# A gated attention and a causal attention with experts on one core: features by halves of the tokens, and half of the gathered work moved into the second part

## What is computed

```python
q, k, v = split(x @ w_qkv.T)                      # 16 heads of 64
dots = einsum('bhid,bhjd->bhij', q, k) * 64**-0.5
gate = soma_gate(q.mean(axis=heads))              # layer norm over 64, linear, gelu, linear,
                                                  # top 32 of 512 tokens per batch kept, sigmoid
dots = dots * (gate[:, None, :, None] * gate[:, None, None, :])
x = layernorm(x + softmax(dots) @ v @ w_out.T + b_out)
```

```python
x1 = x + mla(rmsnorm(x, g1))       # 16 heads of 8, keys and values through a latent of 64, causal softmax
x2 = x1 + moe(rmsnorm(x1, g2))     # 8 experts of 256, top 2 by gate logits, silu
x = layernorm(x + x2)
```

## Time and profile before

| | us |
|---|---|
| three runs | 715.31, 706.88, 701.70 (median 706.88) |
| profiled execution | 699.82, span 698.1 |
| busy: PE, DVE, ACT, POOL | 645.9, 491.2, 419.5, 256.5 |
| mean granted clock of PE | 0.976 |
| end of part one (last matmul, last copy) | 73.4, 73.8 |

### The profile page before, as it was taken

One profiled execution on the slowest core, in us unless ns is written; L12 is line 12 of the kernel. 1 busy time (PEld: TensorE's weight loads), 2 busy tenths in 40 slices (PEclk: granted clock), 3 DMA queues, 4 the chain that ended last, 5 costly groups with the idle time before them and its releaser, 6 DMA issues.

```text
span 698.1 us, 13992 instructions
## 1 busy us (share of the span) xinstructions
PE 645.9 (93%) x5388; PEld 429.9 (62%) x5388; DVE 491.2 (70%) x1043; ACT 419.5 (60%) x753; POOL 256.5 (37%) x321
## 2 busy tenths in 40 slices
PE   7689689889899999999999999999999999989985
PEld 2367444455456666666666766767676667756765
DVE  2557456865777778877887788768777877764775
ACT  2543254666577666766685768666857575664432
POOL 3632301221243344343532543343334343533433
PEclk9899798999999999999999999999999999999999
DMA  8500000000000000000000000000000000000000
GB/s 318 178 0 32 1 1 1 2 1 1 1 1 2 1 1 1 16 2 1 1 17 1 1 2 16 1 1 3 16 1 1 2 17 1 1 1 16 1 16 15
DMA packets 9923, 12.15 MB, mean 17 GB/s; under 512 B 1593, under 2 KB 8194, under 8 KB 9602
## 3 DMA queue, kind: packets, MB, share of 16 engines
q1 hardware_dynamic: 9106, 11.25, 4.8%
q10 hardware_dynamic: 752, 0.01, 0.1%
HBM read 9.16 MB, written 2.10 MB: 16 GB/s over the span
## 4 chain that ended last, share of the span: by engine, by line
PE 69%; DVE 10%; ACT 5%; issue 3%; POOL 2%; POOLq 0%; ACTq 0%; DVEq 0%
PE turn L964 15%; PE turn L957 11%; PE psV L1017 11%; PE psW L1005 9%; PE psS L990 6%; PE turn L919 5%; PE turn L909 3%; DVE negmax L1198 3%; PE psS L979 2%; ACT prob L1117 2%; PE turn L927 2%; ACT X L1036 1%; PE turn L938 1%; DVE qs L1207 1%; PE turn L872 1%
## 5 line engine op out<-in xcount | busy, mean ns | idle before, releaser
L1117 ACT ACTIVATE prob<-psW 128x1024 f32<-128x1024 f32 (+1 forms) x192 | 182.9, 953 | 109.5 <-PE psW L1005 109.1
L1198 DVE TENSOR_REDUCE negmax<-psS 128x2 f32<-128x1024 f32 (+2 forms) x249 | 198.7, 818 | 31.5 <-PE psS L990 31.0
L841 POOL TENSOR_SCALAR_AFFINE_SELECT prob<-prob 128x512 f32<-128x512 f32 x128 | 80.0, 638 | 280.0 <-ACT prob L1117 280.0
L1258 DVE SCALAR_TENSOR_TENSOR late<-late,turn 128x512 f32<-128x512 f32 x128 | 87.5, 684 | 66.3 <-ACT late L1087 65.6
L964 PE MATMUL turn<-wexp,late 128*128 128x128 f32 x1024 | 128.0, 278 | 1.5 <-DVE late L1258 1.3
L964 PEld LDWEIGHTS turn<-wexp,late 128*128 128x128 f32 x1024 | 119.6, 192 | 9.6 <-issue 6.0
L1087 ACT ACTIVATE late<-turn 128x512 f32<-128x512 f32 x128 | 76.4, 598 | 60.7 <-PE turn L957 57.9
L1005 PE MATMUL psW<-qT,kT 26*128 26x256 f32 (+2 forms) x512 | 93.1, 400 | 8.9 <-ACT prob L1117 8.1
L849 POOL TENSOR_TENSOR late<-late 128x512 f32<-128x512 f32 x63 | 80.6, 1280 | 45.7 <-DVE late L1277 45.7
L979 PE MATMUL psS<-kT,qT 24*128 24x256 f32 (+1 forms) x498 | 90.7, 400 | 1.7 <-DVE negmax L1198 1.6
L1017 PE MATMUL psV<-prob,va 128*32 128x512 f32 (+3 forms) x1024 | 91.0, 450 | 0.2 <-POOL prob L841 0.2
(11 more groups left out here) (260 smaller groups left out, 900.8 us busy)
## 6 DMA issues: line engine op xcount, KB each, us to landing
XT<-in_xT SPq DMA_DIRECT2D x4, 512.0 KB, 6.7
X<-in_x SPq DMA_DIRECT2D x1, 2048.0 KB, 15.8
out<-late SPq DMA_DIRECT2D x8, 256.0 KB, 2.2
WQKV<-in_wqkvT SPq DMA_DIRECT2D x1, 1024.0 KB
late<-in_w SPq DMA_DIRECT2D x1, 1024.0 KB, 9.6
WQKV<-in_wqkvT SPq DMA_DIRECT2D x2, 256.0 KB, 3.7
late<-in_woutT SPq DMA_DIRECT2D x1, 512.0 KB
base_all<-base_rows SPq DMA_DIRECT2D x1, 512.0 KB, 3.8
```

What stands on the lines that cost most here:

```text
L841: pool.affine_select(out=blk, in_=blk, compare_op=ALU.is_ge, fill=0.0, base=0, pattern=[[0, 4], [1, P]], channel_multiplier=-1).then_inc(s ...
L1117: A(into, src, ACT.Exp).then_inc(s["exp_ready"], 1)
L1198: last = V.tensor_reduce(negmax[:, u % 2, c, 2 * p:2 * p + 2], scores_in(b, n)[:, :, HALF * i:HALF * i + P * (c + 1)], AX, ALU.max, negate ...
L1258: V.scalar_tensor_tensor(out=hid[:, e % 2, k, :], in0=tanh[:, n % 2, :], scalar=1.0, in1=bank("hidden", b, n)[:, :], op0=ALU.add, op1=ALU. ...
```

## The change

In part one:

- Features are made in eight passes of 256 columns: first the first 256 tokens of all four pairs of batches, then the others. Each half has banks of its own for squares and gate. The square root, reciprocal and product of the first half stand between passes.
- gcol and w1raw come first among the small loads and have a semaphore of their own (`ld_w1`, `w1_ready`). PE's sum of squares waits for neither.
- One square root on a dummy element is issued on ACT before the passes. The ten unread matmuls beside the softmax go, twelve (`IN_GATE`) come ahead of the scores.
- The gather's first half is followed at once by its base rows, queries, keys and scores; the second half of the gather and the values, slots and base rows follow beside the softmax. Base rows go through DRAM in two halves of four batches, each with its semaphores.
- The base rows of batches 3, 5, 6 and 7 are added on POOL, the others on DVE.
- The second half's queries, keys and values leave part one.

In part two, they come as six steps "half parts" right after the first "apply": four of four matmuls, two of one, each copied out by ACT. To keep what they read alive, `WQKV`, `XT`, `Xg` and `Xc` are laid into the tile `prob`. The second "apply" comes behind them. `ADD_AT` goes from 2.02 to 1.32, some other places move by up to 1.4 slots, one "unread" goes, and the last batch's last two experts (before: the last) are summed on DVE alone.

```diff
+WARM, IN_GATE, BY_POOL = 7, 12, (3, 5, 6, 7)
 # SP
-            sp.dma_start(keep["rows"], base[:, :]).then_inc(base_out, 16)
-            sp.wait_ge(base_out, 16)
-            sp.dma_start(base_all[:, :, :], keep["rows"].unsqueeze(0).broadcast_to([P, B, D])).then_inc(base_in, 16)
+            for n in range(NH):
+                rows = slice(HB * n, HB * n + HB)
+                sp.wait_ge(base_sb, n + 1)
+                sp.dma_start(keep["rows"][rows, :], base[:, n, :]).then_inc(base_out[n], 16)
+                sp.wait_ge(base_out[n], 16)
+                sp.dma_start(base_all[:, rows, :], keep["rows"][rows, :].unsqueeze(0).broadcast_to([P, HB, D])
+                             ).then_inc(base_in[n], 16)
 # POOL
-            pool.wait_ge(wc_ready, 2)
+            pool.wait_ge(w1_ready, 1)
...
-            pool.wait_ge(base_in, 16)
             pool.wait_ge(bdT_ready, 1)
-            for b in range(BY_DVE, B):
+            for b in BY_POOL:
+                pool.wait_ge(base_in[b // HB], 16)
 # PE
+            for t in range(B):
+                h, j = divmod(t, B // 2)
+                if t >= 1 and t + 1 < B:
+                    features(t + 1)
+                pe.wait_ge(f_sb, 2 * t + 2)
+                mm(var_in[h][rows_of(j), 0:HALF], ones64[:, :], sq[:, t % 2, 0:HALF], start=True, stop=True,
+                   tile_position=(0, 2 * GH * j)).then_inc(v_done, 1)
+                if t == 1:
+                    pe.wait_ge(w1_ready, 1)
+                if t:
+                    gate_rows(t - 1)
...
             pe.wait_ge(ld_w, 48)
...
+            pe.wait_ge(masks, 2)
+            pe.wait_ge(g_used, 1)
+            unread(IN_GATE)
             for i in range(2):
                 pe.wait_ge(gelu, i + 1)
...
+            gather(0)
+            pe.wait_ge(xs_sb, 1)
+            base_rows(0)
+            for g in range(4):
+                for k in range(4):
+                    last = mm(bank[g][:, P * k:P * k + P], WQKV[:, at:at + P], Xg[:, 0:P], start=True, stop=True)
+                last.then_inc(qk_ps, 1)
...
+            pe.wait_ge(w1_scaled, 1)
+            gather(1)
+            for k in range(2):
+                mm(bank[(6, 4)[k]][:, :], Xc[:, 0:P], WQKV[:, 2 * INNER + 512 * k:2 * INNER + 512 * k + 512],
+                   start=True, stop=True).then_inc(v_ps, 1)
             for n in range(NH):
-                last = mm(bank[(4, 6)[n]][:, :], selh[:, n, :], slot[:, :], start=True, stop=True)
+                last = mm(bank[2 + n][:, :], selh[:, n, :], slot[:, :], start=True, stop=True)
             last.then_inc(sr_ps, 1)
             pe.wait_ge(base_sb, 1)
-            values(0, (bank[7], bank[5]))
-            other = [bank[k] for k in (2, 3, 0, 1)]
-            queries_keys(1, other, range(2))
-            pe.wait_ge(s_shift, 1)
-            queries_keys(1, other, range(2, 4))
-            pe.wait_ge(qk1_sb, 1)
-            for i in range(IN_SOFTMAX):
-                mm(bank[2][:, :], keep["identb"][:, :], keep["maskb"][:, :], start=True, stop=True)
+            pe.wait_ge(xm_ready, 1)
+            base_rows(1)
             pe.wait_ge(bdT_ready, 1)
...
-            values(1, (bank[4], bank[6]))
 # places in part two (some)
-GATE_AT, SUM_AT, ADD_AT = 1.0, 1.21, 2.02
+GATE_AT, SUM_AT, ADD_AT = 1.0, 1.21, 1.32
-EARLY = {0: -40.35, 1: -38.0}
+EARLY = {0: -40.35, 1: -37.2}
+    ("half parts", 0): -40.25, ("half parts", 1): -40.15, ("half parts", 2): -40.05, ("half parts", 3): -39.95,
+    ("half parts", 4): -39.85, ("half parts", 5): -39.75,
-("half turned", 1): 11.5
+("half turned", 1): 13.5
 # the new step on PE
+                elif what == "half parts":
+                    if n < 4:
+                        for k in range(4):
+                            at = P * (4 * n + k)
+                            last = mm(into[:, P * k:P * k + P], WQKV[:, at:at + P], Xg[:, P:2 * P], start=True, stop=True)
+                    else:
+                        last = mm(into[:, :], Xc[:, P:2 * P], WQKV[:, 512 * n:512 * n + 512], start=True, stop=True)
+                    last.then_inc(is_full(*step), 1)
 # POOL's adds and DVE's sums
-                elif what == "add" and (b, n) != (B - 1, NE - 1):
+                elif what == "add" and (b < B - 1 or n < NE - 2):
-                    if (b, n) == (B - 1, NE - 1):
+                    if b == B - 1 and n >= NE - 2:
```

More of the change, by code:

```diff
@@ L298, in _ @@
             last.then_inc(wvo_ps, 1)
-            pe.wait_ge(ld_next, 16 * len(keep["loads"]))
-            mm(bank[5][:, 0:2 * D], keep["wd"][:, :], keep["wu"][:, :, :], start=True, stop=True).then_inc(wqk_ps, 1)
-            def unread(count):
-                for i in range(count):
-                    mm(bank[6][:, :], keep["identb"][:, :], keep["maskb"][:, :], start=True, stop=True)
-            pe.wait_ge(masks, 2)
             for i in range(TOPK // 8):
@@ L716, in causal_attention_and_experts @@
         negmax = sb("negmax", [P, 2, C, 4])
[L717 removed]
+        prob, WQKV, Xg, Xc = (keep[n] for n in ("prob", "WQKV", "Xg", "Xc"))
         oT = sb("oT", [P, NG, T])
@@ L887, in _ @@
                     pe.wait_ge(s["half_T"], 2)
+                    for i in range(4, 6):
+                        wait_free(pe, "half parts", 0, i)
                     for k in range(H):
@@ L1038, in _ @@
                     last.then_inc(s["x_ready"], 1)
+                elif what == "half parts":
+                    wait_full(act, what, 0, n)
+                    if n < 4:
+                        A(QK1[:, 4 * n:4 * n + 4, :], bank(what, 0, n)[:, :].rearrange("p (k t) -> p k t", k=4), ACT.Copy,
+                          scale=DH ** -0.5 if n < 2 else 1.0).then_inc(is_free(what, 0, n), 1)
+                    else:
+                        A(V1[:, 512 * (n - 4):512 * (n - 4) + 512], bank(what, 0, n)[:, :],
+                          ACT.Copy).then_inc(is_free(what, 0, n), 1)
                 elif what == "half exponentials":
```

283 lines of the change are left out of this document (141 added, 142 removed).

## The result

The changed kernel took **695.56 us** (median of six runs, 694.67 to 696.66), the kernel before 704.43 beside it (six runs, 700.4 to 715.31). The ratio is 0.9867, with a 95% interval of 0.983 to 0.9904: some 1.3% faster, inside what the forecast called no change. Profiled executions: 699.82 us before (span 698.1), 694.79 after (span 692.7), so 5.0 us between these two and 8.9 between the medians. Runs far above the others of the same kernel (715.31 us here; 791.0 in "no gate fill", where it was the profiled one, so that kernel has no trace that can be used; 872.0 in "base early"; a few of 711 us and more) are left out of all ratios (without the 715.31 the median of the kernel before is 701.98, and the difference 6.4) and of the medians and ranges of the experiments.

A forecast was written before the change was run, and what follows sets the result against it. TensorE was taken as busy from 200 to 600 us, so most gains lay before about 92 us: 3.8 + 3.5 + 0.4 - 1.0 + 0.8 + 0.7 = 8.2 us, 699.8 to 691.6, scaled to 696; range 686 to 708.

The forecast's parts named there:

- the last of its own signs of being wrong: Whole kernel: the prediction called itself wrong if the clock's falls came elsewhere than it expected; no size given.
- Its other two: Signs of being wrong: feature passes taking over 1.9 us each, or PE waiting for selects in the body.
- rival (b): Start: the twelve unread matmuls run at half clock and give the first gain back; 3.9 gained, 700 us; chance 0.13.
- Start, +3.8: Start to scores: earlier weights and shorter passes bring the scores' end from 29.74 to 25.9 us, 3.8 us gained.
- Gather to delta, +3.5: Part one's end: half-gather chains come earlier, POOL's adds end the part at 70.3 instead of 73.76; 3.5 us gained.
- Half parts and clock, +0.4 - 1.0: Part two's start: half parts fill the idle stretch, 0.4 us gained; a clock fall, weighed 6 in 10, costs 1.0.
- Rival (c): Part two's start: the half parts run at half clock throughout; 3.4 us gained, 701 us; chance 0.12.
- Body, +0.8: Body: one unread pair fewer (0.43) and one wait behind DVE (about 0.4) gone; 0.8 us gained, bounds 0 and 1.5.
- Tail, +0.7: Tail: the seventh expert's add leaves POOL, one gate comes 0.86 us earlier; 0.7 us gained, bounds 0.3 and 2.
- Rival (a): No unread wait, fast broadcast, no fall at part two's start, none at 116 us: 15.8 us gained, 688; chance 0.2.
- Rival (d): Body: POOL waits in early adds for DVE, holding up selects PE needs; 9.6 us slower, 714 us; chance 0.05.
- The scale: Whole kernel: 691.6 us for the profiled execution was scaled to the middle of four runs, 704.3, giving 695.9 us.

The follow-up runs named there:

- no gate fill: The changed kernel without the twelve unread matmuls ahead of the scores; 695.09 us, ratio 0.9867 to the kernel before.
- base early: The changed kernel with the second half's base rows computed ahead of the slots' product instead of behind it; 691.31 us, ratio 0.9841 to the kernel before.
- only loads: The kernel before with only the gate's first weights and their scale loaded ahead of its small columns, nothing halved; 700.28 us, ratio 0.9959.
- gate late: The changed kernel with the gate's first weights waiting for all small loads again, and the first squares behind them; 700.98 us, ratio 0.9958 to the kernel before.
- old places: The changed kernel with part two's steps at their places from before, half parts staying; 697.61 us, ratio 0.9907 to the kernel before.
- end fill: The changed kernel with eight unread matmuls behind part one's last product; 692.76 us, ratio 0.9844 to the kernel before.
- values late: The changed kernel with the half parts' two values products moved behind the first batch's projection; 694.55 us, ratio 0.9885 to the kernel before.
- gather whole: The changed kernel with the gather's second half moved back directly behind the first, none beside the softmax; 695.37 us, ratio 0.9891 to the kernel before.
- before, filled: The kernel before with ten pairs of unread matmuls in TensorE's idle stretch ahead of the first tokens' transposes; 706.19 us, ratio 1.0046.
- base and DVE: The changed kernel with the second half's base rows ahead of the slots' product and one POOL base add given to DVE; 690.36 us, ratio 0.9837.

## Why the prediction was right, step by step

696 against 695.56: the number is right, and most of its terms are not. Two errors of over 3 us cancel, which is luck. By the last of its own signs of being wrong, falls of the clock elsewhere, its mechanism failed: they came at 42 to 46, 58 to 62, 82 to 90 and 666 us as well as at part two's start. Its other two did not show: the passes took 1.49 us, and PE did not wait for selects.

**The sum was 3.2 us too good.** It gave 691.6 for the profiled execution, which took 694.8. (The recorded working has small slips: the items of the start sum to 19.5, not 19.3; 691.6 on its scale is 696.05, not 695.9; the 4.3 of rival (b) follows from none of its figures, 3.8 and a loss of 1.0 being 4.8.)

- *Start, +3.8, measured +4.46.* The pass (1.45) was right at 1.49; ACT's third pass came at 11.10 and not 10.5, and the chain to the Gelu (23.2) ended at 23.92. The assumption that the transposes are held until X has landed, at 21.2, failed: they began at 20.64 without a wait, with X on its way until about 21.5 (issued at 5.02, 16.5 us). In only loads a wait of 1.93 us for `bout` ended at 20.48. Rival (b), half clock in the unread ones, did not occur. But the prediction ascribed the gain to the halving and the loads together, with a reciprocal hidden behind the passes; only loads and gate late show it to be the loads'.
- *Gather to delta, +3.5, measured +1.31.* That POOL ends the part was right: forecast 70.3 less 3.8, 66.5, measured 67.77. The missing 2.2 us are 1.56 for the fall in queries and keys, 0.36 because POOL ends 9.71 us behind the turned weights and not 70.3 - 60.95 = 9.35, and 0.2 in the change of parts. The fall in the outputs (4.97 - 3.33 = 1.64) cost nothing, since POOL came last even so: old places, end fill, gate late and values late have the outputs at 3.33, and from their turned weights to part two it is 10.11 to 10.26 us, here 10.23. The step that failed is that falls of the clock were weighed at part two's start alone.
- *Half parts and clock, +0.4 - 1.0, measured -2.53.* The transposes were late by 0.42 us at full clock (7.62 for 7.20), forecast 0.3. The fall at the start came and cost 9.26 - 7.62 = 1.64 (forecast 1.7 at 6 in 10). The projection gave nothing: of its 2.4 us the forecast counted 0.7, and met a wait of 1.90 us for DVE behind POOL's root. Gather whole shows it without the first fall: 19.30 us from part two to the first causal scores against 18.88 before, so the +0.4 was -0.4. The rest is a further fall, at 82 to 90 us. Rival (c), half clock throughout, did not occur.
- *Body, +0.8, measured +1.27 and +2.90.* The forecast counted one wait of PE behind DVE, about 0.4, and one unread pair. The waits for `qs` recur from batch to batch, 3.5 us in six visits before and 1.2 in two after, and none of the moved places was priced for them: this is the term that was mis-sized. What of the 1.27 ahead of the first tTh is places and what is clock stays open; there the kernel before has falls at 114 to 121 and 186 to 190 us, the changed one only at 110 to 118.
- *Tail, +0.7, measured -2.0.* A fall at 666 us cost 1.1 us in one group and more in those behind it. It is no accident of this one trace: all nine traces with the new places have a fall that starts between 662 and 673 us, and take 44.7 to 45.0 us from the last tTh to the end; the kernel before took 42.73 without a fall there, and 44.25 as only loads, with one. What sets it off, no run shows. The shorter chain of the last two experts is there, but half of what was forecast: from DVE's sum of the sixth expert to POOL's last root it is 7.71 us and was 8.04. From that root to the end it is 5.37 us and was 4.74, which no run explains.
- Rival (a) did not come together: the unread matmuls held the scores back by 0.33 us (23.92 to 24.25), the broadcast of 256 KB took 3.2 us on the page where 2.9 was assumed, the clock fell at part two's start, and a fall stands at 110 to 118 us where one stood at 114.
- Rival (d), adds ahead of selects, did not occur: POOL still idles 251.6 us before its selects, and from 200 to 600 us PE waits for none of them.

**The scale was wrong in kind.** The sum was multiplied by 704.3 / 699.8, which added 4.3 us, as if the scatter of the kernel before belonged to any kernel. It does not. In 46 of the 56 runs of the kernel before beside the experiments, on three chips, time and granted clock lie near a line, 687.1 + 553 (1 - clock) us, with a correlation of -0.93, from 698.5 us at 0.978 to 709.6 at 0.960; the profiled execution, at 0.976, was one of the best. (A line through all 56, which go up to 718.4 us at 0.948, gives 699.5 us at a clock of 0.977, nearly the same.) The changed kernel's six lie at 0.976 to 0.977. At a clock of 0.977 the line gives 699.8 us for before, against 695.3 for after: **at equal clock the changed kernel is 4.5 us faster, and the other 4.4 of the 8.9 between the medians go with the clock, which the runs of the kernel before have lower.** How large that rest is depends on the runs that one takes: the median of the 46 is 703.5, and then it is 3.4; without the 715.31 above it is 1.9. What gives the changed kernel its steady clock stays open. Gate late (0.971 to 0.977), old places (0.974 to 0.979) and gather whole (0.976 to 0.981) are narrow, only loads (0.964 to 0.977) and before, filled (0.962 to 0.978) wide. But base early (0.971 to 0.984) and base and DVE (0.969 to 0.984) are as wide, with halved features and half parts in them, and most of these kernels have three or four runs.

At equal clock the parts of the change are then: the loads 2.5 to 3.4 us (only loads, gate late), the places in part two 2.8 (old places). Each is known to about 1 us. Together they are more than the 4.6 of the whole, so the rest of the change, the gather and the half parts, shows no net gain in these runs: of its 1.31 us at part two's start nothing is left at the first causal scores. The line takes every low clock as equally dear, which it is not: from 76 to 80 us the kernel before had it while PE idled, and in the changed kernel most of it stands under long products.

## What to carry to other kernels

Scale a sum by the profiled execution's own clock, not by the median: ask first what part of the scatter the granted clock explains, and whether the changed kernel will have it. Compare experiments at equal clock too: end fill's 2.8 us by the medians were nothing at equal clock, and gate late's 5.4 were 3.4. A step moved under cover pushes what stood there: write down what is next in line under the cover (here the base rows and their DMA) and what waits for that. The order of small loads was worth more (2.5 to 3.4 us of the time at equal clock, over 4 us at the scores) than the rearranged passes behind them (0.1 to 0.4 us at the scores), so price such parts one by one. An unread matmul that keeps the clock up at the end of a part can itself become what ends the part.

## What the hardware showed unexpectedly

- The clock fell with PE busy 2.00 of 2.00 us, at 58 to 62 us in the changed kernel, behind products of the forms 8*128, 128*4 and 1*4 and with no idle time on PE since 50 us, not only behind idle stretches; and in base and DVE it stayed at half for 14 us under a PE that was busy for most of it. The forecast had tied the fall at part two's start to idle time, though it had noted the one at 116 us as without a long wait ahead. The Trainium skill, "TensorE: Matmul & The Clock Gate", section "What's actually happening", says that activity releases the throttle; in these rows a PE that this profile shows as busy did not keep it released.
- Filling one idle stretch raised the clock there each time (7.62 for 9.26 us, 3.08 for 4.93), but the trace of end fill has more falls further on: summed over the windows of 2 us, (1 - granted clock) x 2 us comes to 12.0 us up to 200 us in it and in the changed kernel alike. Whether the filling moved them is not shown, since each kernel has one trace. At equal clock end fill won nothing, and before, filled lost 1.6 us.
- The same instructions up to the gather gave 3.76 and 6.93 us for it in two kernels, and gather whole's one piece ran at full clock. The profiled execution of base and DVE has a mean clock of 0.969, its three other runs 0.981 to 0.984. So a fall that is seen in one trace needn't have its cause in the step where it stands, nor come again in the next execution.
